# Cross-attention: two sums built by DMA in turn, reciprocals folded to 8 columns, the shift spread from SBUF, ten additions on VectorE

## What is computed

```python
x = _layernorm(builder_state, g1, beta1)
base_n = _layernorm(base_state, g1, beta1)
x = residual + _mha(x, base_n, W_qkv, b_qkv, W_o, b_o)
xn = _layernorm(x, g2, beta2)
U = (xn @ W_in.T + b_in) @ Bmat
# states: s = silu(s @ A.T) + u_t, one after the other
ssm_out = jnp.einsum('tbs,sh->bth', states, Cmat)
return residual + ssm_out + mod   # mod: mean of ctxb @ W_prog.T + b_prog
```

## Time and profile before

| | us |
|---|---|
| median of 3 runs | 2392.19 |
| lowest, highest | 2388.37, 2397.55 |
| the profiled execution | 2392.14 |
| its span | 2390.3 |
| PE busy in it | 2316.8 (97%) |
| DVE busy | 1664.5 (70%) |
| ACT busy | 1118.6 (47%) |
| POOL busy | 1633.1 (68%) |

### The profile page before, as it was taken

The page is one execution under the profiler, slowest core; times in us unless marked ns, Lnnn a source line. Parts: engine busy times, 40 slices in busy tenths (PEclk is TensorE's granted clock), DMA queues, the critical chain, the costliest instruction groups (busy, mean ns, idle before and its releaser), DMA issues.

```text
span 2390.3 us, 36564 instructions
## 1 busy us (share of the span) xinstructions
PE 2316.8 (97%) x14634; PEld 1348.0 (56%) x14634; DVE 1664.5 (70%) x2129; ACT 1118.6 (47%) x1429; POOL 1633.1 (68%) x975
## 2 busy tenths in 40 slices
PE   7999989999999999999999999999999999999987
PEld 7998855555555555455455445554555455445764
DVE  5765547777777777777777777777777777764745
ACT  3653434444444444444444444444444444443554
POOL 1200038888888888888888888888888888886311
PEclk9999999999999999999999999999999999999986
DMA  6660225555555555555555655555555555666623
GB/s 231 196 198 10 80 71 112 118 119 120 115 123 116 131 136 129 130 121 117 124 123 136 143 135 130 121 118 115 115 119 120 118 122 115 150 144 164 206 96 141
DMA packets 130155, 306.57 MB, mean 128 GB/s; under 512 B 10241, under 2 KB 49793, under 8 KB 129346
## 3 DMA queue, kind: packets, MB, share of 16 engines
q0 software_dynamic: 46080, 167.79, 36.0%
q1 hardware_dynamic: 83906, 136.45, 16.4%
HBM read 87.54 MB, written 48.89 MB: 57 GB/s over the span
## 4 chain that ended last, share of the span: by engine, by line
PE 60%; POOL 15%; DMA 14%; issue 7%; DVE 2%; ACT 1%; POOLq 0%; SPq 0%; ACTq 0%; DVEq 0%
PE ps L1153 17%; POOL accp L463 13%; DMA accd<-pt 11%; PE ps L1050 6%; PE ps L1136 4%; PE ps L1138 4%; PE ps L1140 4%; PE ps L1014 4%; PE ps L1210 3%; PE ps L1032 3%; PE ps L1143 3%; PE ps L1022 3%; PE ps L1265 1%; POOL accd L474 1%; PE ps L996 1%
## 5 line engine op out<-in xcount | busy, mean ns | idle before, releaser
L463 POOL TENSOR_TENSOR accp<-accp,pt 128x1024 f32<-128x1024 f32 x512 | 1301.1, 2541 | 44.8 <-ACT pt L612 16.0
L785 DVE TENSOR_REDUCE mx_part<-ps 128x2 f32<-128x1024 f32 x768 | 939.1, 1223 | 451.4 <-PE ps L1050 451.4
L612 ACT ACTIVATE pt<-ps 128x1024 f32<-128x1024 f32 x800 | 779.6, 1022 | 937.8 <-PE ps L1143 920.1
L1153 PE MATMUL ps<-pt,v 128*64 128x512 f32 x3328 | 805.6, 605 | 0.0
L1153 PEld LDWEIGHTS ps<-pt,v 128*64 128x64 f32 x3328 | 201.8, 136 | 362.8 <-issue 315.9
L1050 PE MATMUL ps<-kk,qh 64*128 64x512 f32 x1536 | 346.1, 445 | 18.7 <-DVE mx_part L785 18.7
L1050 PEld LDWEIGHTS ps<-kk,qh 64*128 64x128 f32 x1536 | 143.7, 183 | 359.4 <-DVE mx_part L785 272.3
L1136 PE MATMUL ps<-qh,kk 64*128 64x512 f32 x1664 | 334.4, 397 | 1.7 <-ACT pt L612 1.7
L1140 PE MATMUL ps<-ql,kk 64*128 64x512 f32 x1664 | 329.3, 391 | 0.0
L1138 PE MATMUL ps<-qh,kk 64*128 64x512 f32 x1664 | 329.2, 391 | 0.0
L474 POOL DMA_DIRECT2D accd<-pt x256 | 228.9, 894 | 125.2 <-DMA accd<-pt 83.0
(11 more groups left out here) (146 smaller groups left out, 1851.1 us busy)
## 6 DMA issues: line engine op xcount, KB each, us to landing
accd<-pt POOLq DMA_DIRECT2D x288, 512.0 KB, 4.5
q_scratch<-kk SPq DMA_DIRECT2D x32, 512.0 KB, 4.1
shb<-m_scratch SPq DMA_DIRECT2D x32, 512.0 KB, 6.5
accd<-accp POOLq DMA_DIRECT2D x32, 512.0 KB, 4.9
o_scratch<-ost SPq DMA_DIRECT2D x32, 512.0 KB, 2.8
og<-o_scratch SPq DMA_DIRECT2D x32, 512.0 KB, 4.8
xs<-x SPq DMA_DIRECT2D x16, 512.0 KB, 6.5
qh<-q_scratch SPq DMA_DIRECT2D x32, 256.0 KB, 6.7
```

The costliest lines, as they stand in the source:

```text
L463: nc.gpsimd.tensor_tensor(acc[:, :], acc[:, :], pt[n % PT_SLOTS][:, :], ALU.add).then_inc(added_p, 1)
L612: nc.scalar.activation(pt[n % PT_SLOTS][:, :], src, ACT.Exp, scale=SCALE).then_inc(exped, 1)
L785: nc.vector.tensor_reduce(mx_part[:, m % QT, :, m // QT], src, AX_X, ALU.max).then_inc(max_taken, 1)
L1153: ins = mm(ps[HD * h:HD * (h + 1), 6, :], v[:, t, f:f + HD], pt[n % PT_SLOTS][:, h * QB:(h + 1) * QB], start=(t == 0), stop=(t == NT - 1))
```

## The change

- *Ten additions on VectorE*: `V_STEPS` becomes 2 to 11. In such a step TensorE first writes the shift pair of the even tile, then the odd tile complete without a shift, then the other three pairs of the even tile. In the other steps the shift pair comes first too, but for tile 0.
- *Two sums by DMA in turn*: seven tiles go to `acca`, five to `accb`, alternately, and POOL adds the other 14. At the unit's end POOL adds `accb` to `accp` (`add_b`), then sends `accp` to `acca`. Tile buffers are six instead of seven.
- *Reciprocals folded*: ScalarE copies the sums out of PSUM (`take_den`, step 4), two DMAs fold the two rows of 512 to 128 partitions x 8 columns, VectorE takes one reciprocal (step 6), it is stored to DRAM and spread by two DMAs to `rdenb`, and POOL scales the output behind tile 18 instead of VectorE.
- *The shift straight from SBUF*: `spread_shift` issues two DMAs, one for each head, that read one row of `sh` 128 times. There is one `shb` instead of two, and SyncE waits for the last addition of the unit before. SyncE's queue has the fold and the spread of the reciprocals ahead of `store_o`.
- *Prologue*: group 1 of x is loaded ahead of the weights, both first groups get their statistics together, ScalarE scales the weights before it normalises group 0, the bias product and the first projections are cut so that transposes lie between.
- In the last part the steps for the reciprocals and the modulation come one or two groups `d` later.

```diff
-D_TILES = [2, 5, 8, 11, 13, 16, 19, 21, 24]
-P_TILES = [t for t in range(NT) if t not in D_TILES]
-PT_SLOTS = 7
-
-V_STEPS = [2, 3, 7, 8, 9, 10, 11]
+A_TILES = [1, 5, 9, 13, 17, 21, 24]
+B_TILES = [3, 7, 11, 15, 19]
+P_TILES = [t for t in range(NT) if t not in A_TILES + B_TILES]
+P_SUMS = len(P_TILES) + 1
+PT_SLOTS = 6
+
+V_STEPS = [2, 3, 4, 5, 6, 7, 8, 9, 10, 11]
...
             def spread_shift(w):
                 sp.wait_ge(shift_ready, w + 1)
-                wait(sp, shb_loaded[w % 2], 16 * (w // 2))
-                sp.dma_start(m_scratch[w % 2], sh[w % 2][0:HD + 1:HD, :].bitcast(F32)).then_inc(sh_stored, 16)
-                sp.wait_ge(sh_stored, 16 * (w + 1))
-                wait(sp, shifted, len(V_TILES) * (w - 1))
-                sp.dma_start(shb[w % 2][:, :, :], m_scratch[w % 2:w % 2 + 1].to_broadcast([P, 2, QB]))\
-                    .then_inc(shb_loaded[w % 2], 16)
+                wait(sp, shifted, len(V_TILES) * w)
+                for h in (0, 1):
+                    src = sh[w % 2][HD * h:HD * h + 1, :].bitcast(F32).rearrange("o k -> o () k")
+                    sp.dma_start(shb[:, h, :], src.to_broadcast([1, P, QB])).then_inc(shb_loaded, 16)
+
+            def fold_den(u):
+                sp.wait_ge(den_taken, u + 1)
+                for h in (0, 1):
+                    sp.dma_start(den8[HD * h:HD * (h + 1), :],
+                                 den_sb[HD * h:HD * h + 1, :].rearrange("o (p j) -> o p j", j=8)).then_inc(den8_loaded, 16)
+
+            def spread_rden(u):
+                sp.wait_ge(rden_ready, u + 1)
+                sp.dma_start(r_scratch[u % 2].rearrange("h (p j) -> (h p) j", j=8), rden8[:, :]).then_inc(rden_stored, 16)
+                sp.wait_ge(rden_stored, 16 * (u + 1))
+                wait(sp, o_scaled, u)
+                for h in (0, 1):
+                    sp.dma_start(rdenb[HD * h:HD * (h + 1), :], r_scratch[u % 2, h:h + 1].to_broadcast([HD, QB]))\
+                        .then_inc(rdenb_loaded, 16)
...
-            load_xs(0)
+            for n in (0, 1):
+                load_xs(n)
             sp.dma_start(w3[:, 0], w_qkv_t[:, 0]).then_inc(w_loaded[0], 16)
...
                 if u > 0:
+                    fold_den(u - 1)
+                    spread_rden(u - 1)
                     store_o(u - 1)
...
+            def add_b(u):
+                acc = accp[u % 2]
+                pool.wait_ge(added_b, 16 * len(B_TILES) * (u + 1))
+                pool.wait_ge(added_p, P_SUMS * (u + 1) - 1)
+                nc.gpsimd.tensor_tensor(acc[:, :], acc[:, :], accb[:, :], ALU.add).then_inc(added_p, 1)
...
+            def scale_o(u):
+                pool.wait_ge(rdenb_loaded, 32 * (u + 1))
+                pool.wait_ge(o_taken, u + 1)
+                nc.gpsimd.tensor_tensor(oraw[:, :], oraw[:, :], rdenb[:, :], ALU.mult).then_inc(o_scaled, 1)
...
+                    if t == 18 and u > 0:
+                        scale_o(u - 1)
                     if t == 22 and u > 0:
                         low_o(u - 1)
...
+                add_b(u)
                 send_sum(u)
...
+            def take_den(u):
+                act.wait_ge(sum_spread, u + 1)
+                wait(act, den8_loaded, 32 * u)
+                nc.scalar.activation(den_sb[0:HD + 1, :], ps[0:HD + 1, 7, :], ACT.Copy).then_inc(den_taken, 1)
...
-            def invert(u, i):
-                dve.wait_ge(sum_spread, u + 1)
-                c = slice(i * P, (i + 1) * P)
-                nc.vector.reciprocal(ps[:, 7, c], ps[:, 7, c]).then_inc(rden_ready, 1)
-
-            def scale_o(u):
-                dve.wait_ge(rden_ready, 4 * (u + 1))
-                dve.wait_ge(o_taken, u + 1)
-                nc.vector.tensor_tensor(oraw[:, :], oraw[:, :], ps[:, 7, :], ALU.mult).then_inc(o_scaled, 1)
+            def invert(u):
+                dve.wait_ge(den8_loaded, 32 * (u + 1))
+                wait(dve, rden_stored, 16 * u)
+                nc.vector.reciprocal(rden8[:, :], den8[:, :]).then_inc(rden_ready, 1)
...
             pe.wait_ge(cols_loaded, 16)
-            bias(0)
+            bias(0, range(3))
             turn(0)
+            bias(0, range(3, FC))
             for n in range(NG):
-                if n + 1 < NG:
+                if 1 < n < NG - 1:
                     turn(n + 1)
...
+                    if n < 2:
+                        project_q(n, range(2))
+                        turn(n + 1)
+                        project_q(n, range(2, FC))
+                    else:
+                        project_q(n, range(FC))
...
-                    scores(u, 2 * j + 1 if j in V_STEPS else 2 * j)
+                    if j in V_STEPS:
+                        open_tile(u, 2 * j)
+                        shift_scores(u, 2 * j, True)
+                        open_tile(u, 2 * j + 1)
+                        scores(u, 2 * j + 1, True, True)
+                    else:
+                        score_tile(u, 2 * j)
...
-                    scores(u, 2 * j if j in V_STEPS else 2 * j + 1)
+                    if j in V_STEPS:
+                        scores(u, 2 * j, False, True)
+                    else:
+                        score_tile(u, 2 * j + 1)
```

More of the change, by code:

```diff
@@ L507, in _ @@
                 if d == 8:
+                    scale_o(UNITS - 1)
+                if d == 10:
                     low_o(UNITS - 1)
@@ L630, in _ @@
                         take_o(u - 1)
+                    if j == 4 and u > 0:
+                        take_den(u - 1)
                     if j == 10 and u > 0:
@@ L873, in low_wo @@
                     .then_inc(wo_lo, 1)
-            def between(u, j):
-                if j in V_STEPS:
-                    add_shift(u, 2 * j + 1)
-                if u > 0 and j in (4, 5):
-                    invert(u - 1, 2 * (j - 4))
-                if u > 0 and j == 6:
-                    scale_o(u - 1)
-            def behind(u, j):
-                if u > 0 and j in (4, 5):
-                    invert(u - 1, 2 * (j - 4) + 1)
             for u in range(UNITS):
@@ L898, in _ @@
                         row_max(u + 1)
-                    behind(u, j)
+                    if u > 0 and j == 6:
+                        invert(u - 1)
                     if u == UNITS - 1 and j < 3:
@@ L999, in turn, with bias @@
                         ins.then_inc(turned, 1)
-            def bias(w):
+            def bias(w, columns):
                 pe.wait_ge(w_loaded[w], 16)
-                for m in range(FC):
+                for m in columns:
                     for k in range(FC):
@@ L1006, in bias, with project_q @@
                                  start=(k == 0), stop=(k == FC - 1))
-                ins.then_inc(bias_mm, 1)
-            def project_q(n):
+                if FC - 1 in columns:
+                    ins.then_inc(bias_mm, 1)
+            def project_q(n, chunks):
                 pe.wait_ge(n_ready, 2 * (n + 1))
-                for c in range(FC):
+                for c in chunks:
                     wait(pe, q_ready, FC * (n - 1) + (c + 1))
@@ L1061, in turn_max @@
                 pe.wait_ge(max_ready, w + 1)
-                wait(pe, o_scaled, w - 1)
+                wait(pe, den_taken, w - 1)
                 for q in range(QT):
@@ L1086, in _ @@
                         pe.wait_ge(bias_ready, 1)
-                        bias(1)
-                        bias(2)
+                        bias(1, range(FC))
+                        bias(2, range(FC))
                     if n == 3:
@@ L1121, in _, with open_tile, shift_scores, scores @@
             pe.wait_ge(ones_set, 2)
[L1124 to L1127 removed]
+            rows = (slice(0, HD), slice(HD, 2 * HD))
+            def open_tile(u, t):
+                if t == 0:
+                    pe.wait_ge(qh_loaded[u % 3], 16 * (u // 3 + 1))
+                    pe.wait_ge(ql_loaded[u % 2], 16 * (u // 2 + 1))
+                wait(pe, exped, NT * u + t - 1)
+            def shift_scores(u, t, first):
                 if t == 0:
                     pe.wait_ge(shift_ready, u + 1)
[L1130 to L1136 removed]
+                for h, r in enumerate(rows):
+                    ins = mm(ps[:, 2 * (t % 2) + h, :], ones_row[r, :], sh[u % 2][r, :], start=first, stop=not first)
+                if not first:
+                    ins.then_inc(scored, 1)
+            def scores(u, t, first, last):
+                p, b, key = k_slot(u), 2 * (t % 2), slice(t * P, (t + 1) * P)
+                for h, r in enumerate(rows):
+                    mm(ps[:, b + h, :], kk[r, p, 0, key], qh[u % 3][r, :], start=first, stop=False)
                 for h, r in enumerate(rows):
@@ L1139, in scores, with score_tile @@
                 for h, r in enumerate(rows):
-                    ins = mm(ps[:, b + h, :], kk[r, p, 0, key], ql[u % 2][r, :], start=False, stop=t in V_TILES)
-                if t not in V_TILES:
-                    for h, r in enumerate(rows):
-                        ins = mm(ps[:, b + h, :], ones_row[r, :], sh[u % 2][r, :], start=False, stop=True)
```

(12 more changed lines are left out.)

141 lines of the change are left out of this document (80 added, 61 removed).

## The result

The changed kernel takes 2770.35 us (median of 4 runs, 2761.66 to 2776.24) against 2394.87 us for the kernel before: a ratio of 1.158 with a 95% interval of 1.156 to 1.160. The forecast was 2352 us, with a range up to 2560. So it missed on both the sign and the range. The case that the range left out, the two halves of the shift one behind the other, had been priced at 2765 us.

What follows compares the result with a forecast made beforehand. TensorE was taken as the bound, with POOL close behind. Pairs -21.5, disturbances -15, reciprocals +1, prologue -5 and last part 0 sum to -40.5 us, from 2392.1 to about 2352 us; range 2338 to 2560.

Steps and rivals of the forecast that it cites:

- The case that the range left out: Shift's two 256 KB halves run in turn, landing at 24.2 us, 12.9 too late: +413 us, 2765 us; chance 0.18.
- the term for the shift straight from SBUF: One hop instead of two, landing 6.5 us after issue; cover grows from 0.4 to some 4 us, counted within the -15.
- the first rival: Shift spread: one SBUF partition feeds slowly, 11.1 us per half, giving 2410 us (both at once) or 2765 (in turn); chance 0.30.
- The point of decision: Shift's landing time: from 11.3 us on, when VectorE's first addition wants it, the slow-partition rival decides.
- the sign: Evidence that would show the forecast wrong: accumulating DMAs landing much above 4.5 us while the shift is under way.
- three pairs less a unit: Loop: three more VectorE additions spare TensorE three `ones_row` pairs of 0.23 us in each of 32 units; -21.5 us.
- disturbances: Loop: TensorE's stops, taken as 19 us in all, of which POOL's relief removes 15; bounds 0 and 19.
- reciprocals: Folded reciprocals in each unit: added copies, DMAs and waits are hidden; counted +1 us, bounds 0 and +6.
- prologue: Before the loop: first projection starts at about 19.8 us instead of 25.06 and the gain stays; -5 us, bounds 0 and -7.
- last part: After the loop: reciprocals and scaling leave VectorE, modulation steps move two groups later; 0 us, bounds -2 and +2.
- The rival that the disturbances stay: Loop: only TensorE's pairs go, ScalarE waits for buffers as landings stretch; 2366 us, or 2382 if units lose more; chance 0.14.
- VectorE as the bound: Steps with an addition: VectorE's loop paces them; 0.1 us longer means 32 us and 2384 us; chance 0.04.

Runs made afterwards that it cites:

- the single DMAs: Kernel before with awaited 256 KB DMAs added behind its last store: one SBUF row read 128 times 11.1 us, rows 0 and 64 together 18.9 us.
- the shift by way of memory: Changed kernel with only the shift sent through DRAM again (4 KB store, then one load spread to 128 partitions): 2368.36 us, ratio 0.990.
- spare reads: Changed kernel with the shift through DRAM, plus unneeded 128-times reads of a row of `sh` each unit: one read 2491.68 us, two 2718.96 us.
- the one with seven additions: Changed kernel with the shift through DRAM and VectorE's additions at steps 2, 3, 7 to 11 instead of ten: 2390.66 us, ratio 1.000.
- a version at 2347.0 us: Changed kernel with the shift through DRAM, last-part fold and following steps moved later, and `norm_scale(2, 3)` moved back in the prologue: 2347.0 us, ratio 0.982.

## Why the prediction was wrong, point by point

**The step that failed** is the term for the shift straight from SBUF. No row showed a DMA that reads one partition 128 times, and I priced it by the row of the broadcast from memory, 6.5 us, and let that stand for the likeliest value. It takes 11.1 us for one half; for both, 18.9 us in the single DMAs and 19.5 in the unit shown (the longest landing of a half is 22.1). And it holds what other queues have under way meanwhile, which was in no term. The estimate under the first rival was nearly exact (11.1 us per half; 24.2 in turn with the 2 us of latency), and the case in turn is what came. What was wrong is the weight: 0.18 for that case, on the ground that one row of memory is read at full speed. That row speaks of memory and not of the source that the change uses. The range could have held the result only by reaching to that case.

**The price of the rival was right for the wrong reason.** It said 12.9 us too late in every unit, +413 us. The unit did lose 12.7 us (68.93 - 56.23). But VectorE was only 8.1 us late, since the halves flow a little faster than estimated; the rest is a further wait, for ScalarE, and TensorE's lower clock after each stop. In numbers: TensorE waits (250.4 + 46.7)/31 = 9.6 us a unit, and the remaining 3.1 us are matmuls at 0.43 instead of 0.23 us a pair. The windows bear that out: TensorE's busy time is 431.35/500 x 68.93 = 59.5 us a unit, against 499.33/500 x 56.23 = 56.2 for the same matmuls with the shift by way of memory, 3.3 us more. The Trainium skill's rate (SBUF — State Buffer, section "Door 1: The DMA port swizzle") had given an estimate of 2670 us, 100 us too little. It puts the halves at 9.6 us each, which the 9.58 us of the bench bears out, and the shift 9.9 us too late; what is missing, 3.1 x 31 = 96 us, is the size of the clock's part.

**The point of decision was incomplete.** I took the 11.3 us until VectorE wants the shift as the cover. That wait did come, in every unit, and it is what TensorE stood behind. But with the addition three steps later 361 of the 402 us stay, and with spare reads that nobody waits for most of it comes back. A second cover counts as much, that of POOL's DMAs: tile 24 and the sum, and six buffers of 12.4 us. Even one slow read, which VectorE does not wait for at all, costs 3.7 us a unit. I had written down the sign (landings of the accumulating DMAs much above 4.5 us while the shift is under way) but had put no price on it.

**The rest of the sum**, read from the profiled executions of the kernel before, of the version by way of memory and of the one with seven additions:

| part | forecast, us | measured, us | from |
|---|---|---|---|
| three pairs less a unit | -21.5 | -21.7 | loop 1764.7 -> 1743.0 |
| disturbances | -15 | -18.9 | loop 1783.6 -> 1764.7 |
| reciprocals | +1 | in the line above | |
| prologue | -5 | +2.6 | first `sh` 330.8 -> 333.4 |
| last part | 0 | +16.4 | last `sh` to the end, 275.9 -> 292.3 |
| sum without the shift | -40.5 | -21.6 | span 2390.3 -> 2368.7 |
| the shift from SBUF | in the -15 | +402 | 2368.36 -> 2770.35 |

Each measured value is of one execution, and 13 executions of the kernel before lie between 2383 and 2400 us, so a few us in a line may be chance. The -21.6 us lie within the bounds that the prediction added up (-50 to -12), but are only about half of its -40.5, because the prologue and the last part went the other way. The reciprocal of 8 columns takes 0.19 us where 0.1 had been taken, and TensorE waits for nothing of it in the loop. The pairs and the disturbances came as worked out; the unit is 56.23 us where 56.3 had been forecast. The rival that the disturbances stay is refuted, and so is VectorE as the bound: the pace of the steps didn't change. The prologue's first step was right (19.23 us, forecast 19.8). "What follows is paced by TensorE and keeps it" was not: I had not followed the one instruction that the diff moves, `norm_scale(2, 3)`, to what is queued behind the engine that waits for it. The last part was wrong in the same manner. I wrote "past loads with room", but had looked at where steps move to and not at what is queued behind SyncE's new wait. Both were worth what I had given them once the order was right: 4.8 us in the prologue and +1.5 us in the last part, in a version at 2347.0 us where the forecast was 2352.

**What stays open.** The 3.1 us a unit put down to the clock are read from the traces and were not tested by themselves, since no run stopped TensorE without holding the DMAs. Nor was the order in which a DMA engine works off its packets tested. The kernel before loses 448 us by the same lines and the changed one 402. Its unit grows by 71.66 - 57.54 = 14.1 us, that of the changed kernel by 12.7, and 31 x 1.4 = 44 us is nearly all of the difference. The 2.1 us by which its shift is issued later, less the 0.6 us of disturbances that the kernel before had already, are of that size; no run tests it.

## What to carry to other kernels

Spread a row from memory and not from SBUF, where this case is any guide: reading one partition of SBUF 128 times saves a hop and takes 11.1 us where the row in memory takes 3.3, and a second such read comes on top. Price a slow DMA by what else the 16 engines carry meanwhile, and not only by who waits for its result: look for a window with a high DMA share and few GB/s. A moved wait is followed down its own queue to the first instruction behind it that another engine needs.

## What the runs showed of the hardware that I had not expected

- One partition of SBUF read 128 times: 256 KB in 11.1 us, against 2.3 us from 128 partitions and 3.3 us from one row of memory. Two such reads issued together take 18.9 us even from rows 0 and 64.
- While they run, the DMA engines show 91% busy at 32 GB/s, and accumulating DMAs from POOL's queue, with other sources, take 18.9 instead of 5.7 us (two spare reads a unit).
- Even issuing is held: SyncE's next DMA behind two such reads keeps its queue for 7.0 us (median of 32, changed kernel) or 8.5 us (two spare reads), against 0.45 us with the shift by way of memory.
- After TensorE had stood for 8 us its granted clock was 0.60 on average over the next 8 us, and 1.00 again in the window from 1050 to 1060 us. Before, with 7 us idle in 500, it was 1.00.
